# Linear-attention block on one core: a running maximum that is 256 wide in place of 512, and two transposes a block in place of four

## What is computed

```
xg = group_norm(x, 32 groups)
q, k, v = split(xg @ W_qkv)             # each 4096 x 256
k = softmax(k over the 4096 tokens)
context = k^T v                         # 256 x 256
out = x + (q context) @ W_out + b_out
```

## Time and profile before

| | us |
|---|---|
| median of 3 runs | 1262.89 (1261.8 to 1263.22) |
| the profiled execution, its own time | 1263.93 |
| its span, from the first to the last instruction | 1262.2 |
| PE busy | 1220.6 (97%) |
| DVE busy | 879.4 (70%) |
| ACT busy | 839.1 (66%) |
| POOL busy | 657.4 (52%) |

### The profile page before, as it was taken

The page is one execution under the profiler, slowest core; times in us unless marked ns, Lnnn a source line. Parts: engine busy times, 40 slices in busy tenths (PEclk is TensorE's granted clock), DMA queues, the critical chain, the costliest instruction groups (busy, mean ns, idle before and its releaser), DMA issues. The chain is left out here.

```text
span 1262.2 us, 21236 instructions
## 1 busy us (share of the span) xinstructions
PE 1220.6 (97%) x8396; PEld 1132.2 (90%) x8396; DVE 879.4 (70%) x1264; ACT 839.1 (66%) x1139; POOL 657.4 (52%) x284
## 2 busy tenths in 40 slices
PE   3899999999999999999999999999999999999998
PEld 3798999989999898999989999899999989999886
DVE  5877767877677776767777577676776777577461
ACT  4476857767576776857767576775756768576663
POOL 7274653836546374553736547364563736537320
PEclk9899999999999999999999999999999999999999
DMA  8247657486665867657486564866657576573523
GB/s 332 85 167 267 215 192 245 151 300 217 215 220 170 281 200 258 204 185 260 163 294 209 206 227 157 293 217 236 203 180 265 185 271 219 190 241 118 190 92 134
DMA packets 109107, 266.69 MB, mean 211 GB/s; under 512 B 12240, under 2 KB 12240, under 8 KB 109008
## 3 DMA queue, kind: packets, MB, share of 16 engines
q1 hardware_dynamic: 109008, 265.34, 62.1%
HBM read 198.18 MB, written 67.11 MB: 210 GB/s over the span
## 5 line engine op out<-in xcount | busy, mean ns | idle before, releaser
L283 POOL TENSOR_TENSOR xt_lo<-xt_raw,xt_hi 128x1024 fp32r<-128x1024 f32 x128 | 307.0, 2401 | 496.1 <-ACT xt_hi L543 462.3
L289 POOL TENSOR_TENSOR x_lo<-x_raw,x_hi 128x1024 fp32r<-128x1024 f32 x128 | 324.3, 2548 | 67.5 <-ACT x_hi L548 67.4
L594 ACT ACTIVATE o_stage<-ps_e,bias 128x512 f32<-128x512 f32 x256 | 172.8, 689 | 125.6 <-PE ps_e L463 125.6
L770 DVE TENSOR_TENSOR e_lo<-e_raw,e_hi 128x1024 fp32r<-128x1024 f32 x128 | 251.6, 1966 | 3.1 <-ACT e_raw L561 2.2
L739 DVE TENSOR_TENSOR mx<-ps_k,mx 128x512 f32<-128x512 f32 x224 | 154.7, 691 | 120.6 <-ACT e_raw L552 108.5
L552 ACT ACTIVATE e_raw<-ps_k 128x512 f32<-128x512 f32 x256 | 142.1, 596 | 131.6 <-PE ps_k L328 131.6
L328 PE MATMUL ps_k<-wk_hi,xt_hi 128*128 128x256 f32 x1024 | 214.5, 291 | 3.8 <-DVE wk_lo L725 3.0
L328 PE MATMUL ps_k<-wk_lo,xt_hi 128*128 128x256 f32 x1024 | 207.2, 284 | 0.0
L560 ACT ACTIVATE e_hi<-e_raw 128x1024 fp32r<-128x1024 f32 x128 | 135.0, 1055 | 66.7 <-PE ps_g L409 36.8
L698 DVE BATCH_NORM_STATS2 bn<-xs 128x6 f32<-128x512 f32 x240 | 153.4, 686 | 35.3 <-DMA xs<-in_xt_dram 34.9
L328 PEld LDWEIGHTS ps_k<-wk_hi,xt_hi 128*128 128x128 f32 x1024 | 166.7, 191 | 12.5 <-issue 4.0
(11 more groups left out here) (81 smaller groups left out, 1875.2 us busy)
## 6 DMA issues: line engine op xcount, KB each, us to landing
xt_raw<-in_xt_dram SPq DMA_DIRECT2D x128, 512.0 KB, 4.6
x_raw<-in_xn_dram SPq DMA_DIRECT2D x128, 512.0 KB, 3.4
out_dram<-o_stage SPq DMA_DIRECT2D x256, 256.0 KB, 4.6
xs<-in_xt_dram SPq DMA_DIRECT2D x240, 256.0 KB, 5.0
w_setup<-in_w_dram SPq DMA_DIRECT2D x2, 256.0 KB, 9.7
wk<-in_w_dram SPq DMA_DIRECT2D x1, 256.0 KB, 9.8
wq_t<-in_w_dram SPq DMA_DIRECT2D x1, 256.0 KB, 9.8
b_col<-in_b_out_dram SPq DMA_DIRECT2D x1, 1.0 KB, 9.9
```

Of the source, the lines that this page charges most:

```text
L283: nc.gpsimd.tensor_tensor(xt_lo[:, s], xt_raw[:, s], xt_hi[:, s].bitcast(F32), ALU.subtract).then_inc(xt_lo_ready, 1)
L289: nc.gpsimd.tensor_tensor(x_lo[:, s], x_raw[:, s], x_hi[:, s, :, 0:C].bitcast(F32), ALU.subtract).then_inc(x_lo_ready, 1)
L594: nc.scalar.activation(o_stage[:, q % O_SLOTS, :], ps_e[:, h, :], ACT.Identity, bias=bias[:, h:h + 1]).then_inc(o_ready, 1)
L770: nc.vector.tensor_tensor(e_lo[:, j], e_raw[:, j], e_hi[:, j % E_SLOTS].bitcast(F32), ALU.subtract).then_inc(e_lo_ready, 1)
```

## The change

The buffer `mx` is one running maximum, 256 wide. DVE folds tile by tile: each half is now two instructions of 256 elements in place of one of 512, each waiting for the one before it; the first tile of a block is the copy. TensorE turns `mx` with two transposes and not four, and `block_max` reduces 256 elements per partition and not 512. The counts in the waits on `max_done` follow (32 folds an image in place of 16); which chunk or half is waited for is the same as before.

```diff
-        mx = sb("mx", [P, 2 * C])
+        mx = sb("mx", [P, C])
@@ keys_high
-                        pe.wait_ge(max_done, b * (2 * NCH) + (2 * j - 2))
+                        pe.wait_ge(max_done, b * (TILES * NCH) + TILES * (j - 1))
@@ turn_max
-                pe.wait_ge(max_done, b * (2 * NCH) + (NCH * blk + NCH))
+                pe.wait_ge(max_done, b * (TILES * NCH) + TILES * HALF * (blk + 1))
                 for d in range(CB):
-                    for h in range(2):
-                        last = nc.tensor.transpose(to[:, 0, (2 * d + h) * P:(2 * d + h + 1) * P],
-                                                   mx[:, h * C + d * P:h * C + (d + 1) * P], ident)
+                    last = nc.tensor.transpose(to[:, 0, d * P:(d + 1) * P], mx[:, d * P:(d + 1) * P], ident)
@@ key_max
                 dve.wait_ge(k_out, b * (2 * NCH) + (2 * j + h + 1))
-                if j % HALF == 0 and h == 0:
-                    if j or not (isinstance(b, int) and b == 0):
-                        dve.wait_ge(t_ps, b * 2 + j // HALF)
-                    nc.vector.tensor_copy(mx[:], ps_k[:, j % 2, h, :]).then_inc(max_done, 1)
-                    return
-                dve.wait_ge(max_done, b * (2 * NCH) + (2 * j + h))
-                nc.vector.tensor_tensor(mx[:], ps_k[:, j % 2, h, :], mx[:], ALU.max).then_inc(max_done, 1)
+                for t in (2 * h, 2 * h + 1):
+                    tile = ps_k[:, j % 2, h, (t % 2) * C:(t % 2 + 1) * C]
+                    if j % HALF == 0 and t == 0:
+                        if j or b:
+                            dve.wait_ge(t_ps, b * 2 + j // HALF)
+                        nc.vector.tensor_copy(mx[:], tile).then_inc(max_done, 1)
+                    else:
+                        dve.wait_ge(max_done, b * (TILES * NCH) + (TILES * j + t))
+                        nc.vector.tensor_tensor(mx[:], tile, mx[:], ALU.max).then_inc(max_done, 1)
@@ block_max
-                nc.vector.tensor_reduce(m_blk[:, blk, :], src[:, 0, :].rearrange("p (d n) -> p d n", d=CB),
+                nc.vector.tensor_reduce(m_blk[:, blk, :], src[:, 0, 0:C].rearrange("p (d n) -> p d n", d=CB),
```

## The result

| | before | after |
|---|---|---|
| median, us | 1262.36 (12 runs, 1260.15 to 1263.94) | 1257.44 (12 runs, 1256.2 to 1260.49) |
| profiled execution, us | 1263.93 | 1256.2 |
| its span, us | 1262.2 | 1254.5 |
| one period, the turn of block 0 of b = 6 to that of b = 7, us | 76.18 | 75.70 |

The ratio is 0.9963, with a 95% interval of 0.9954 to 0.9972: 4.7 us less (3.5 to 5.8). The forecast was 1258.2, a ratio of 0.996.

What follows compares the result with a forecast made beforehand. TensorE's dense stream was taken as the bound from image 1 on, DVE in image 0; -6.5 us over 30 turns and +1.8 us in image 0 gave -4.7, so 1258.2 us from 1262.89; 8-in-10 range 1256.0 to 1261.8.

Steps and rivals of the forecast that it cites:

- The saving on TensorE: Turns of both blocks outside image 0: two transposes fewer save 0.218 us each, 30 turns 6.5 us.
- The fold: DVE's 256-wide fold would take 0.43 us, carried down from 0.691 at 512 and 1.208 at 1024 elements.
- The price between folds: On DVE, 0.105 us behind each fold that waits; a chunk's four folds 2.04 us against 1.49, 0.55 more.
- The cover at the turn of block 0: From when the turn could start after DVE's last fold to its actual start, 0.26 us left; the tight place.
- The other covers: Later keys (microseconds), turn of block 1 (2.1 us), combine steps (0.97 and 1.20 us idle): later DVE wouldn't reach PE.
- x_lo: PE's 0.45 us gather wait on POOL's x_lo would stay as it is, its chain moving forward with PE.
- rival B: x_lo's end doesn't move with PE: 15 x 0.218 = 3.3 us given back, 1261.5 us; chance 0.10.
- Image 0: DVE is the path there: gather 2.2 us later, less 0.43 at block 1's turn, +1.8 us.
- the gather was to start: Image 0's gather 2.2 us later: 0.58 at the block maximum's hand-over plus 3 x 0.55 for chunks 4 to 6.
- the slow turn of block 1: Image 0, PE at half clock: transposes 0.213 us apart, two left out give 0.43 us.
- the clock: Image 0's delayed gather: half-clock stretch of the same length; bounds 1.1 us given back or 1.1 more.

Runs made afterwards that it cites:

- The free folds: 256-wide folds into a 512-wide maximum, four transposes as in the kernel before, each fold waiting for the one two before; 1262.46 us, single run.
- the extra folds: Changed kernel with one or three more folds after the last fold of block 0 in images 1 to 15; 1258.97 us and 1271.75 us.
- The folds alone: Kernel before with 256-wide folds, each waiting for the one before, but four transposes and 512-wide block maximum kept; 1265.15 us, ratio 1.0015.

## Why the prediction was right, and where its terms were off

**The saving on TensorE: right.** 30 x 0.218 = 6.5 us was forecast. At b = 7 the turn of block 1 is 0.21 us shorter to the next matmul (0.43 to 0.22), that of block 0 0.23 (0.36 to 0.13); over 14 periods 6.3 to 6.5 us went, 28 x 0.218 = 6.1 of them forecast; the 0.2 to 0.4 beyond have no cause shown. The 0.109 us a transpose came from start distances and not from the 0.272 of an instruction. The figure of 81 ns from the Trainium skill, "TensorE: Matmul & The Clock Gate", section "Back-to-back issue gap", would have given 4.9 for the 30 turns, as an estimate; the distances after agree with 109 ns, and not with it.

**The fold: 0.43 forecast, 0.424 measured.** The line through 512 and 1024 elements held (0.432); so did (N+151)/0.96 ns (424 at 256) of the Trainium skill, "VectorE: DVE Perf Modes", section "The TRN2 errata — SBUF-src ops pay a fixed extra latency per instruction".

**The price between folds: mis-sized.** I charged 0.105 us behind each fold, 0.55 us more a chunk; measured 0.38. The 0.105 was read where two wait instructions stand in front of a fold; in the changed kernel only one of the three gaps has two, the others have 0.035. The Trainium skill ("VectorE: DVE Perf Modes", section "The DRAIN you can't avoid") says, of copies, that a semaphore in between costs nothing extra. The free folds disagree: 0.33 us apart against 0.46 behind a wait on the fold just ahead. So it was the wait and not the width that cost: four folds of 256 without that wait take 1.42 us, two of 512 with it 1.49.

**The cover at the turn of block 0: right place, larger.** 0.26 forecast, 0.47 measured by the extra folds. The other covers held: no other wait of PE is new in images 1 to 15.

**x_lo: right.** The wait in the gather is where it was, 0.45 before and 0.48 in most images after, where rival B asked for 0.67; so B is out, and it moved with PE.

**Image 0: the sum near, its parts not, and in part by luck.** +1.8 us was forecast. What is left of the measured change is +2.1: the steady part brought 6.3 to 6.5 us in 14 periods and 0.4 behind the last of them (from that turn to the end 82.3 us before, 81.9 after), 6.8 in all, against -4.7; the interval of 1.2 us either way goes with it. The folds alone gave +1.9 (0.8 to 3.0). But the gather was to start 2.2 us later, and at 60.1. It started at 57.73, 57.79 and 58.87. From first fold to gather it went from 31.38 to 32.46 and 32.40, 1.0 to 1.1, and to 31.59 in the profile where slice 11 landed early: the spread of that transfer's landing is as large as the term. The 0.38 a chunk explains the part behind the block maximum (3 x 0.38 - 0.27; measured 13.87 - 12.99 = 0.88).

Against this error of about 1.1 us stand others the other way. The 0.43 us of the slow turn of block 1 was credited in full. In the second profile PE had it (two transposes from 61.35 to 61.78, and no wait behind). In the first and third it waited 0.35 and 1.03 us for the sums mv, which stand on DVE behind the folds of chunk 7 and behind `e_low`, stretched to 2.07 and 2.32 us while POOL's subtraction ran. I had not seen this place. Before, PE reached the sums at 62.28, and DVE had ended them at 61.72 + 0.31 = 62.03: 0.25 us of cover. And the clock: I took a slow stretch of the same length, and PE's work in it was 3.5 us in one execution of the changed kernel and 5.6 in another, so both less and as much as before occurred. That the sum came near the measured one is then partly luck, and how much of the median's +2.1 us is each of these, the runs don't settle.

## What to carry to other kernels

On an engine that is dense, take the price of an instruction from the distance between starts; here 28 x 0.218 = 6.1 us stood against 6.3 to 6.5 measured. On the engine that gets the work, look for the place with the least cover from its last instruction to the reader and test that with extra instructions: here 0.47 us are free and each 0.1 beyond costs 1.5 us. Work that repeats every period may be free in steady state and still cost in the first period, where nothing covers it and what is queued behind it is late.

## What the runs showed that I had not expected

A tensor_tensor with two SBUF operands, 256 wide, took 0.42 us on VectorE with GpSimd idle, and 2.61, 1.59 and 2.03 us when a GpSimd tensor_tensor of 2.4 us had begun before it: it ended 0.3 us after GpSimd's did. Where it began first, by 0.07 us, it took 0.42. The fold that reads PSUM and SBUF kept 0.424 us in the mean of 480, so joining in SBUF what can be folded out of PSUM cost 29 us here. `e_low`, 1.22 us alone, is stretched in the same way, up to 2.43 us in image 0 of the kernel before.

A VectorE instruction of 256 elements starts 0.33 us after the one ahead if its wait is met already, 0.46 if it waits for that one, 0.53 with a second wait instruction in front. TensorE's granted clock fell to 1.2 GHz around the first gather's start in each of the three profiles of the changed kernel (at 58.0, 55.6 and 59.8 us; the gathers began at 57.7, 57.8 and 58.9) and came back 3.4 to 6.8 us later. The clock, the instant of the first fold and the wait on mv go with the 2.5 us by which the first and the third differ; the twelve executions of the first measurement spread over 4.3 us, and for the rest of that there is no trace.
